# Joining the end of an attention layer to the start of the feed-forward layer behind it

## The reference

```
x = x + xattn(layernorm(x), ctx, ctx, mask, Wq..Wo, bq..bo)      # 16 heads of 16
h = layernorm(x)
hq = fake_quant_nvfp4(h, s_in)            # blocks of 16, e4m3 scales, e2m1 values
g, u = hq @ quant(gate_w).T, hq @ quant(up_w).T                  # 256 -> 1024
x = x + fake_quant_nvfp4(silu(g) * u, s_in_down) @ quant(down_w).T   # 1024 -> 256
```

## Time and profile before

| | us |
|---|---|
| median of 3 runs (712.4 to 712.82) | 712.79 |
| the profiled execution's own time | 713.3 |
| its span, first to last instruction | 711.1 |

### The profile page before, as it was taken

How to read it: one execution, slowest core, us unless ns; L and a number is a source line. 1 busy time by engine, 2 the same in 40 slices (tenths; PEclk the granted TensorE clock), 3 DMA queues, 4 the chain that set the end, 5 groups by cost and what they waited for, 6 DMA issues and landing times.

```text
span 711.1 us, 14550 instructions
## 1 busy us (share of the span) xinstructions
PE 567.0 (80%) x4543; PEld 417.5 (59%) x4552; DVE 504.9 (71%) x1418; ACT 378.0 (53%) x717; POOL 213.3 (30%) x243
## 2 busy tenths in 40 slices
PE   5399999609999999966899999996435865778777
PEld 3188888409998998954566666664212443345445
DVE  6358787694655566673556777663769999999987
ACT  1324443113443333324667777767675878785674
POOL 5724774514655455652222333310000000000000
PEclk9689999959999999996999999999667999998899
DMA  8873443269466655607000000000000000000001
GB/s 318 270 229 117 131 150 116 76 221 386 140 221 198 198 177 181 202 29 238 2 1 0 0 0 0 0 2 1 4 1 0 30 15 16 30 29 16 16 30 60
DMA packets 35540, 68.49 MB, mean 96 GB/s; under 512 B 5581, under 2 KB 24542, under 8 KB 34464
## 3 DMA queue, kind: packets, MB, share of 16 engines
q1 hardware_dynamic: 28816, 52.37, 22.4%
q0 software_dynamic: 5520, 13.61, 5.5%
q10 hardware_dynamic: 1152, 1.88, 0.8%
HBM read 53.78 MB, written 15.80 MB: 98 GB/s over the span
## 4 chain that ended last, share of the span: by engine, by line
PE 45%; DVE 22%; ACT 13%; issue 8%; DMA 7%; SPq 3%; POOL 2%; DVEq 0%; POOLq 0%; ACTq 0%
PE quad L1118 10%; PE quad L1183 5%; DVE hh L2223 5%; ACT nPT L869 4%; PE bank L1192 4%; PE bank L1254 3%; PE quad L1467 3%; PE quad L1273 2%; DMA x_after_ffn<-row,niU 2%; PE quad L1296 2%; DVE nM L2069 2%; DMA early<-in_W 2%; ACT hqT L1012 2%; DMA X<-x_after_ffn 2%; PE duo L1307 2%
## 5 line engine op out<-in xcount | busy, mean ns | idle before, releaser
L777 ACT ACTIVATE hid<-quad,early 128x128 f32<-128x128 f32 x156 | 44.6, 369 | 83.5 <-PE quad L1183 83.5
L1183 PE MATMUL quad<-xts,early 128*128 128x128 f32 x624 | 75.4, 280 | 3.5 <-DMA early<-in_W 3.4
L1183 PEld LDWEIGHTS quad<-xts,early 128*128 128x128 f32 x624 | 73.5, 195 | 6.0 <-issue 4.0
L1192 PE MATMUL bank<-W2s,hid 128*128 x312 | 70.5, 379 | 0.0
L1192 PEld LDWEIGHTS bank<-W2s,hid 128*128 128x128 f32 x312 | 57.8, 190 | 7.1
L598 POOL DMA_INDIRECT x_after_ffn<-row,niU x39 | 39.1, 1002 | 57.4 <-DVE row L1849 40.4
L1467 PE MATMUL quad<-uT,xqT 128*128 128x512 bf16 x128 | 39.7, 414 | 17.5 <-DVE hh L2223 16.5
L988 ACT ACTIVATE sil<-quad,gmx 128x512 f32<-128x512 f32 x64 | 41.1, 688 | 20.5 <-PE quad L1458 20.0
L1844 DVE SCALAR_TENSOR_TENSOR row<-bank,sco,row 128x256 f32<-128x256 f32 x39 | 18.6, 476 | 45.9 <-PE bank L1192 45.4
L2069 DVE TENSOR_REDUCE nM<-quad 128x32 f32<-128x2048 f32 x16 | 36.7, 2292 | 18.6 <-PE quad L1273 18.6
L2223 DVE SCALAR_TENSOR_TENSOR hh<-quad,gmx,sil 128x512 f32<-128x512 f32 x64 | 45.1, 744 | 4.8 <-PE quad L1467 4.3
(11 more groups left out here) (365 smaller groups left out, 1326.4 us busy)
## 6 DMA issues: line engine op xcount, KB each, us to landing
early<-in_W SPq DMA_DIRECT2D x37, 514.0 KB, 5.6
row<-rows_by_expert SPq DMA_DIRECT2D x38, 134.0 KB, 2.3
early<-in_ctxO SPq DMA_DIRECT2D x4, 1024.0 KB, 8.0
ctxs<-in_ctxT SPq DMA_DIRECT2D x4, 1024.0 KB, 13.7
W2s<-in_W SPq DMA_DIRECT2D x8, 512.0 KB
X<-x_after_ffn SPq DMA_DIRECT2D x7, 516.0 KB, 7.4
out<-yo SPq DMA_DIRECT2D x14, 256.0 KB, 2.1
early<-in_W ACTq DMA_DIRECT2D x2, 514.0 KB, 8.5
```

Of the source, the lines that this page charges most:

```text
L777: ins = act.activation(hid[:, u, c * P:(c + 1) * P], bank[2 + u][:, c * P:(c + 1) * P], ACT.Gelu, bias=W1r[:, k, DC * H2 + c:DC * H2 + c + 1])
L1183: ins = pe.matmul(bank[2 + u][:, n * P:(n + 1) * P], W1r[:, m % RING, c * H2 + n * P:c * H2 + (n + 1) * P], xt[:, u, c, :], start=c == 0, ...
L1192: ins = pe.matmul(bank[6 + u % 2][:, 0:D], hid[:, u, c * P:(c + 1) * P], W2s[:, bass.ds(ex, 1), c, :].rearrange("p o s -> p (o s)"), start ...
```

## The change

On ACT, done_roots(0) moves up behind the softmax of batch 14; tile_norm is split into rows_normed (four activations) and rows_halved (two). Group 0's rows_normed moves ahead of inverse_sums of batch 15, its rows_halved behind weight tile 3, group 1's rows_normed behind that; weight tile 4, the last roots and the Silu table load follow, then weight tile 5. Group 1's rows_halved moves behind x_out(0). On PE the last projection moves ahead of weight tiles 4 and 5, and the wait for n_ad goes. On DVE done_scales(0) moves ahead of add_rows(14), rows_scaled(0) behind the last statistics, and group 1's block_scales behind the first two products. The barrier moves into the Else branch; single waits take its place (s_wTe for the weights, s_dst, s_wT).

```diff
@@ -817,16 +817,21 @@
                 to = (gT[:, :, 0:512], gT[:, :, 512:1024], uT[:, :, 0:512], uT[:, :, 512:1024], dT[:, :, 0:P], dT[:, :, P:2 * P])[t]
                 act.copy(to, bank[6][:].bitcast(BF16).rearrange("p (c o) -> p c o", c=DC if t < 4 else FT)).then_inc(s_wTe, 1)
 
-            def tile_norm(g, g0):
-
+            def rows_normed(g, g0):
                 for u in range(4):
                     t = g * 4 + (u + 1)
                     ins = act.activation(x4s[g0 % 2][:, u * D:(u + 1) * D], X2[:, bass.ds(t, 1), 0:D].rearrange("p o d -> p (o d)"), ACT.Identity,
                                          bias=nm2[:, bass.ds(t, 1)], scale=rs2[:, bass.ds(t, 1)])
                 ins.then_inc(s_x4, 1)
+
+            def rows_halved(g, g0):
                 act.wait_ge(s_x4, g + 1)
                 act.activation(absx[g0 % 2], top(x4s[g0 % 2]), ACT.Abs)
                 act.copy(xb[g0 % 2], top(x4s[g0 % 2])).then_inc(s_ax, 1)
+
+            def tile_norm(g, g0):
+                rows_normed(g, g0)
+                rows_halved(g, g0)
 
             def done_roots(part):
                 act.wait_ge(s_dst, part + 1)
...
@@ -886,6 +891,11 @@
                     if stage < 2:
                         queries_out(b + 1, 1 - h)
                     exps(b)
+                    if stage == 1:
+                        done_roots(0)
+                    if stage == 2:
+                        act.wait_ge(s_nm2, 4)
+                        rows_normed(0, 0)
                     if stage == 0:
                         rows_norm(b + 2)
                     if stage < 2:
...
@@ -901,10 +911,12 @@
                         weights_out(1 if stage == 1 else 3)
                     if stage < 2:
                         maxima_out(b + 1)
-                    if stage:
-                        weights_out(2 if stage == 1 else 4)
+                    if stage == 1:
+                        weights_out(2)
                     if stage == 2:
-                        weights_out(5)
+                        rows_halved(0, 0)
+                        rows_normed(1, 1)
+                        weights_out(4)
 
                 act.wait_ge(s_nm2, 1)
                 rows_norm(0)
...
@@ -932,13 +944,11 @@
                     batch(i * 2 + 8, 0, p=i + 4, k=i * 2 + 3)
                 batch(NB - 3, 1, p=NB // 2 - 1)
                 batch(NB - 2, 0, p=NB // 2 - 1, stage=1)
-                done_roots(0)
                 batch(NB - 1, 1, stage=2)
-                act.wait_ge(s_nm2, 4)
-                tile_norm(0, 0)
-                tile_norm(1, 1)
                 done_roots(1)
                 done_roots(2)
+                act.activation(tscr[:], tscr[:], ACT.Silu)
+                weights_out(5)
             with act.Else():
                 rows_roots(1)
                 rows_roots(2)
...
@@ -995,8 +1005,8 @@
                 act.wait_ge(s_h, 2 * t + 2)
                 act.copy(hb[:, u * FF:(u + 1) * FF], upper(u)).then_inc(s_ah, 1)
 
-            act.wait_ge(s_cdone, 3)
             x_out(0)
+            rows_halved(1, 1)
             for u in range(4):
                 silu(u, u, first=u < 2)
                 if u:
...
@@ -1340,9 +1350,11 @@
                         maxima_turn(b + 1)
                     if stage == 0:
                         queries(b + 2, 1)
-                    else:
-                        weights_in(2 if stage == 1 else 4)
+                    elif stage == 1:
+                        weights_in(2)
                     if stage == 2:
+                        project(b)
+                        weights_in(4)
                         weights_in(5)
 
                 for c in range(DC):
...
@@ -1363,8 +1375,6 @@
                 batch(NB - 3, 1)
                 batch(NB - 2, 0, stage=1)
                 batch(NB - 1, 1, stage=2)
-                project(NB - 1)
-                pe.wait_ge(n_ad, NB)
             with pe.Else():
                 with pe.Fori(0, NB) as b:
                     for q in range(2):
...
@@ -1437,10 +1447,9 @@
                 pe.wait_ge(s_fin, 2 * NB)
                 for t in range(6):
                     weights_in(t)
-            pe.drain().then_inc(s_cdone, 1)
-
-
-            pe.wait_ge(s_wTe, 6)
+                pe.drain().then_inc(s_cdone, 1)
+                pe.wait_ge(s_cdone, 3)
+
 
             def x_in(g):
                 pe.wait_ge(s_xq, g + 1)
...
@@ -2132,18 +2144,18 @@
                     batch(i * 2 + 7, between=lambda: weight_rounded(i * 2 + 1, stn))
                     stn.leave(SLOTS // 2)
                 batch(NB - 2, between=lambda: done_stats(0))
+                done_scales(done_parts[0], 1, stn)
                 b = NB - 1
                 add_rows(b - 1)
                 new_stats(b - 1)
                 done_stats(1)
-                done_scales(done_parts[0], 1, stn)
                 divide(b)
                 rows_sizes(0, 0, stn)
                 block_scales(rows_c, stn)
-                rows_scaled(0, stn)
                 add_rows(b)
                 stn.link(new_stats(b))
                 done_stats(2)
+                rows_scaled(0, stn)
                 rows_quantised(0, stn)
             with v.Else():
                 stg = Steps(v, s_vg)
...
@@ -2253,10 +2264,11 @@
                 hidden_quantised(1)
                 product(t + 3, 3)
 
+            v.wait_ge(s_wT, 6)
             rows_sizes(1, 1, st)
-            block_scales(rows_c, st)
             product(0, 0)
             product(1, 1)
+            block_scales(rows_c, st)
             rows_scaled(1, st)
             rows_quantised(1, st)
             product(2, 2)
```

More of the change, by code:

```diff
@@ L969, in _ @@
                 tile_norm(0, 0)
-                tile_norm(1, 1)
+                rows_normed(1, 1)
                 done_roots(1)
                 done_roots(2)
-            act.drain().then_inc(s_cdone, 1)
-            act.activation(tscr[:], tscr[:], ACT.Silu)
+                act.activation(tscr[:], tscr[:], ACT.Silu)
+                act.drain().then_inc(s_cdone, 1)
+                act.wait_ge(s_cdone, 3)
             def x_out(g):
@@ L1472, in _ @@
             pe.wait_ge(s_xqe, 1)
+            pe.wait_ge(s_wTe, 4)
             for u in range(4):
@@ L1519, in _ @@
             NGR = NTILE // 4
+            pe.wait_ge(s_wTe, 6)
+            pe.wait_ge(s_dst, 3)
             x_in(1)
@@ L2204, in _ @@
                 rows_quantised(0, stg)
-            v.drain().then_inc(s_cdone, 1)
-            v.wait_ge(s_cdone, 3)
+                v.drain().then_inc(s_cdone, 1)
+                v.wait_ge(s_cdone, 3)
             done_scales(slice(9, NTILE + 1), 3, st)
```

## The result

The changed kernel takes **707.9 us** (median of 12 runs, 706.1 to 711.6); the kernel before took 712.8 beside it (12 runs). The ratio is 0.9927, with a 95% interval of 0.9912 to 0.9941: 0.6 to 0.9% faster, 5 us. The forecast was 707.3, in a range of 705.6 to 709.6. The total lies in the range, but one of its terms is wrong: the head of the first group (from its first gate product to its fourth tile's half) gave back twice what the prediction allowed. The profiled execution took 708.7 (span 706.6).

A forecast was written before the change was run, and what follows sets the result against it. The prediction saw the join as bound by a serial chain on ACT and DVE: x_in 6.8 us earlier, less 1.3 in the first group, takes 5.5 off 713.3, giving 707.8; the median lies 0.5 lower, 707.3 (range 705.6 to 709.6).

The forecast's parts named there:

- The chain on ACT: On ACT up to group 0's halves: absolute values follow weight tile 3 at once, a gain of 5.9 us.
- DVE and the projection: DVE takes 6.96 us to the quantised rows; PE's last projection takes 2.99 and is hidden by 1.3.
- PE's jump: PE's jump over the Else branch takes about 3.45 us, ends at 498.25, nearly tying with the rows; thin cover.
- the forecast of x_in: At the join on PE, x_in starts at 498.7 instead of 505.54, a gain of 6.8 us.
- the rival in which it takes 9: Rival, chance 0.03: PE's jump takes longer; from 9.0 us on the gain is gone, at 11 the kernel takes 714.8.
- ACT at x_out: ACT is free at 499.5 and x_in's result there at 499.8, so x_out(0) has a cover of 0.3 us.
- The rival in which ACT is late: Rival, chance 0.17: ACT's queue or table load delays x_out(0) and all behind it, giving 708.3 to 709.4 us.
- The loss in the first group: In the first group's head, block scales between tiles 1 and 2's products, where DVE has no wait, cost 1.3 us.
- that 0.2 is lost and found again: DVE's first product starts 0.2 us late, regained because the second tile's products wait 0.66 for PE.
- The rival of a quicker clock: Rival, chance 0.15: PE gets 2.4 GHz for x_in and the first gate, up to 0.9 us more: 706.4.
- its own two terms: x_in 6.8 us earlier less 1.3 lost in the first group: the fourth tile's half on ACT starts 5.5 earlier.
- the distance stays: Behind the first group's fourth half nothing changes: the distance from there to the end is as before.

The follow-up runs named there:

- experiment 1: The changed kernel with the barrier put back behind both branches, all moves kept: 708.8 us, ratio 0.9948 to the kernel before.
- experiment 2: The kernel before with only the barrier and PE's wait for the last add_rows taken away, nothing moved: 711.5 us, ratio 0.9986.
- Experiment 3: The changed kernel with the last projection put back behind weight tiles 4 and 5: 711.2 us, ratio 0.9976 to the kernel before.
- experiment 6: The changed kernel with group 1's halves on ACT ahead of weight tile 4, so PE's jump starts later: 708.7 us, ratio 0.9939 to before.
- experiment 7: The changed kernel with 16 unneeded matrix products on PE behind weight tile 5: 707.4 us, ratio 0.9936 to the kernel before.
- experiment 4: The changed kernel with group 1's block scales between the products of tiles 0 and 1: 706.6 us, ratio 0.9912 to the kernel before.
- experiment 5: The changed kernel with group 1's halves behind weight tile 4 on ACT, its maxima, scales and scaling ahead of DVE's first product: 704.3 us, ratio 0.9888.
- experiment 8: The changed kernel with group 1's rows early and 16 unneeded products on PE (edits of experiments 5 and 7): 703.6 us, ratio 0.9873 to before.

## Why the prediction was right, and where it was not

That ACT's early halves set the gain off is read from the two traces; no kernel of the study takes this move alone away. Experiments 1 to 3 show that the barrier is at most a small part of it and that the projection's move is needed beside it.

**The chain on ACT, right.** Absolute values 5.9 earlier, as forecast. The wait for done_scales cost nothing: the normalising ends at 488.14 and the logarithm of inverse_sums (L886) follows at once.

**DVE and the projection, right.** 6.97 against 6.96. The projection ran at 490.26 to 492.26, faster than the 2.99 allowed, and was hidden. Experiment 3 shows that it has to be: without its move x_in is 4.96 later.

**PE's jump, right, with as little cover as forecast.** It took 3.82 and was hidden by 0.2; the forecast of x_in, +15.2, is met within 0.1 (gain 6.91 against 6.8). The 0.4 that I let pass between the jump and x_in is not needed: in experiment 6 it was less than 0.1. That experiment also shows the bound: with the jump's end 1.8 later, x_in moves with the jump. Over the ten profiles the same jump took 3.3 to 3.9, so the rival in which it takes 9 was not seen. The Trainium skill (Runtime: NRT & Kernel Launch, Instruction fetch mechanics) says that a taken branch to a page outside the engine's window must fetch it first. The traces agree: in each of the ten profiles a packet of instructions moves during PE's jump (last section). The price of 3.3 to 3.9 is the trace's.

**ACT at x_out, right.** Cover 0.37 against 0.3. The table load takes 1.28, and the next activation starts 1.30 after the load did: no stop. The rival in which ACT is late did not come about. The Trainium skill (ScalarE: Activation LUTs, What ACT_TABLE_LOAD costs) gives a drain of some 1380 ns beside a load; this load (497.64 to 498.94) shows none.

**The loss in the first group, wrong by half: 1.3 forecast, 2.6 measured.** The step that failed is "that 0.2 is lost and found again: the second tile's products wait 0.66 for PE". I took PE's pace from the rows of before, as if x_in's move carried it along. The block scales cost 1.33, as sized. But PE stays at half its clock longer than before, so that tile 1's products wait 1.36 for it, not 0.66 or less. And the scales, now ahead of tile 2's products, hold PE up for 2.77; behind that its clock falls again (0.64 over the window) and the last up product is late too. That the wait brings this fall is not shown: in experiment 7 a wait of 2.57 at the same place is followed by an up product of 1.26 at the higher clock. These two make 0.54 + 0.43 = 0.97 of the 1.3 that was missed, the later start of the first products the other 0.31. Experiment 2 shows the clock's share without any move (1.1 in the same order of instructions), experiment 7 takes it away (1.7 less for the products), and experiment 4 takes the scales away with what hangs on them (1.88).

**The rival of a quicker clock went the other way**: x_in took 1.04 and the gate 1.49, both at the slow level. PE idled 3.52 ahead of x_in, as the argument against it said.

**Why the sum still fits: in part by luck.** By its own two terms the profiled execution gains 6.9 - 2.6 = 4.3 at the fourth half, not 5.5. From there to the end of the span it took 0.9 less than before (706.6 - 515.75 = 190.9, before 711.1 - 519.37 = 191.7), where the prediction said that the distance stays. Nearly all of this is found in one place, ahead of the products of the last group. From the seventh group's fourth half to DVE's first product behind it, the windows before and after are:

```profile
667.19:680.52 13.33, 11.26 (x71) 8.41 (x73) 10.37 (x15) 7.43 (x9) 0.00 (x0) 0.74 0.06 21
```

```profile
663.45:675.94 12.49, 10.13 (x71) 7.66 (x73) 10.37 (x15) 7.33 (x9) 0.00 (x0) 0.86 0.07 22
```

The instructions are the same and DVE is as busy; PE was granted 0.74 of its clock before and 0.86 after, and the stretch took 0.84 less. The five groups ahead of it keep the same distance in both kernels, 23.7. From the seventh group's fourth half to the last's there are 22.45 before and 20.05 to 21.61 in the nine other profiles, 21.49 in experiment 2, where nothing was moved, and 21.61 in experiment 1, where the barrier is back. So neither the moves nor the barrier alone accounts for it. The prediction had no term for it, and it made up for most of what the head lost beyond the forecast. In all, the profiled execution gained 4.6 and the medians 4.9, where 5.5 was forecast. Whether other executions of the kernel before had this slow stretch no profile shows.

## What to carry to other kernels

When work is moved out of a serial chain, look where it lands: here x_in gained 6.9 and the head behind it gave 2.6 back, half of it through 1.3 us of small instructions that stood in a wait before and in none afterwards, most of the rest through TensorE at half its clock. Put moved work into a wait that the trace shows, and do not take TensorE's pace behind a changed wait from the rows before it (experiments 4 and 5 won back 1.3 and 3.6 us by the medians, the first within the noise). A jump over a branch that does not run can cost microseconds on one engine and nothing on the others, so let it start early, behind the shortest wait that there is.

## What was unexpected of the hardware

The same jump over the Else branch took 3.3 to 3.9 us on PE in every one of ten profiles, while those of ACT and DVE took 34 to 47 ns in the kernel before. Why theirs cost so little no run shows. The DMA records suggest that PE's waits for instructions: in experiment 2, whose jumps of ACT and DVE lie 11 us later, this is all that the instruction queues moved during PE's jump, 490.5 to 494.2 (queue; packets, MB, share of the DMA engines), and nothing in the 3.5 us ahead of it:

```profile
q8 instruction: 1, 0.02, 2.2%
```

In each of the other nine profiles that queue moves one such packet during PE's jump too. PE's array works on beside the jump: in experiment 8 the 16 products ran at 495.92 to 499.32 while the jump ran from 495.6 for 3.62, so they cost no time of x_in's.

The same instructions in the same order took 1.1 us longer in the head of a group because PE was granted 0.50 for 5.5 us on end, where before the clock rose within 4.2 (0.60 over these; experiment 2). Products that nothing needs, put ahead of a stretch, can hold the clock up (experiment 8: 1.00 throughout) or be caught by its fall themselves (experiment 7: 4.52 instead of 3.40 for the same 16).
